# Experts: the front of a chunk runs six steps ahead instead of four

## What is computed

```python
x = x + gnn(...) + mix(...)                        # the residual x2
xf = layernorm(x)
probs = softmax(xf @ Wg + bg)                      # 8 experts
comb = probs * (probs is among the two largest)
out = 0
for e in range(8):
    h = gelu(xf @ W1[e] + b1[e])                   # 512 -> 128
    out = out + comb[:, e:e+1] * (h @ W2[e] + b2[e])   # 128 -> 512
x = x + out
```

## Time and profile before

| | |
|---|---|
| three runs | 2988.32 us median (2987.90 to 2995.39) |
| the profiled execution | 2990.87 us |
| its span in the profile | 2989.3 us |
| busy in the span | PE 2588.8, PEld 2119.4, DVE 1641.8, ACT 1326.5, POOL 1121.3 us |
| mean granted TensorE clock | 0.944 |

### The profile page before, as it was taken

How to read it: one execution, slowest core, us unless ns; L and a number is a source line. 1 busy time by engine, 2 the same in 40 slices (tenths; PEclk the granted TensorE clock), 3 DMA queues, 4 the chain that set the end, 5 groups by cost and what they waited for, 6 DMA issues and landing times.

```text
span 2989.3 us, 78905 instructions
## 1 busy us (share of the span) xinstructions
PE 2588.8 (87%) x32457; PEld 2119.4 (71%) x32457; DVE 1641.8 (55%) x3354; ACT 1326.5 (44%) x3694; POOL 1121.3 (38%) x1128
## 2 busy tenths in 40 slices
PE   5989998999999999589897788888888589589998
PEld 4867886888887888465686677777776465477776
DVE  5225777666666666647313455555555646666643
ACT  3323443656565655322331465665555322334432
POOL 0000001777776767100001477777777211122110
PEclk8999999999999999899998899999999889699998
DMA  5662013999999999540126599999999641122211
GB/s 198 229 266 101 36 54 105 354 355 356 350 358 343 357 340 346 177 129 2 71 95 233 210 345 352 349 351 356 354 345 351 208 118 52 39 96 92 71 64 57
DMA packets 233911, 647.37 MB, mean 217 GB/s; under 512 B 39072, under 2 KB 45856, under 8 KB 231491
## 3 DMA queue, kind: packets, MB, share of 16 engines
q0 software_dynamic: 137088, 466.78, 42.9%
q1 hardware_dynamic: 96451, 175.38, 17.1%
HBM read 551.60 MB, written 116.19 MB: 223 GB/s over the span
## 4 chain that ended last, share of the span: by engine, by line
PE 68%; DMA 15%; DVE 7%; issue 5%; POOL 2%; ACT 2%; SPq 1%; POOLq 0%; DVEq 0%; ACTq 0%
PE ps L1282 10%; PE ps L1312 5%; PE ps L1325 5%; DMA Y<-KVd,srcE 5%; PE ps L595 4%; PE ps L596 4%; PE ps L597 4%; DMA xT<-KVd,srcE 3%; PE ps L1289 3%; PE ps L1006 2%; PE ps L1008 2%; PE ps L1007 2%; DMA Qd<-stage 2%; PE ps L1966 2%; PE ps L1968 2%
## 5 line engine op out<-in xcount | busy, mean ns | idle before, releaser
L1189 POOL DMA_INDIRECT Y<-KVd,srcE x356 | 341.1, 958 | 132.7 <-issue 63.9
L1189 POOL DMA_INDIRECT xT<-KVd,srcE x225 | 214.6, 954 | 312.6 <-DVE xs L1053 195.4
L1482 ACT ACTIVATE stage<-ps,stage 128x128 f32<-128x128 f32 x832 | 294.9, 367 | 32.8 <-PE ps L1289 29.8
L1463 ACT ACTIVATE work<-ps 128x512 f32<-128x512 f32 x309 | 180.4, 597 | 285.6 <-PE ps L1282 285.3
L595 PE MATMUL ps<-Wh,xs 128*128 128x512 f32 x600 | 240.3, 400 | 55.4 <-DVE xs L535 55.4
L1463 ACT ACTIVATE G<-ps 128x512 f32<-128x512 f32 x315 | 183.4, 597 | 233.2 <-PE ps L1282 232.8
L1382 DVE COPY G<-ps 128x512 f32<-128x512 f32 x208 | 143.9, 692 | 259.5 <-PE ps L1289 251.0
L1282 PE MATMUL ps<-ident,Y 128*128 128x128 f32 x1424 | 201.6, 280 | 42.7 <-DMA Y<-KVd,srcE 34.3
L596 PE MATMUL ps<-Wl,xs 128*128 128x512 f32 x600 | 238.1, 397 | 0.0
L597 PE MATMUL ps<-Wh,xs 128*128 128x512 f32 x600 | 237.9, 396 | 0.0
L1189 POOL DMA_INDIRECT WA<-KVd,srcE x120 | 116.8, 974 | 318.7 <-PE ps L597 276.4
(11 more groups left out here) (403 smaller groups left out, 6884.3 us busy)
## 6 DMA issues: line engine op xcount, KB each, us to landing
KVd<-stage SPq DMA_DIRECT2D x96, 256.0 KB, 2.0
xTd<-xT SPq DMA_DIRECT2D x2, 6250.0 KB, 26.4
xT<-xTd SPq DMA_DIRECT2D x2, 6250.0 KB, 26.4
aggd<-work SPq DMA_DIRECT2D x6, 2048.0 KB, 7.4
Qd<-stage SPq DMA_DIRECT2D x48, 256.0 KB, 2.0
G<-aggd SPq DMA_DIRECT2D x48, 256.0 KB, 2.7
Y<-in_x SPq DMA_DIRECT2D x4, 1536.0 KB, 14.5
G<-mixq SPq DMA_DIRECT2D x24, 256.0 KB
```

The source lines that it names most:

```text
L1189: pool.indirect_dma_start(out=kvs[a], out_offset=None, in_=KVd[l][:, :], in_offset=bass.IndirectOffsetOnAxis(ap=srcE[:, n:n + 1], axis=0)) ...
L1463: act.activation(kT[n % len(kT)], banks(l)[place_of(l, "k", n) % len(banks(l))][:, :], ACT.Copy).then_inc(out_a, 1)
L1482: last = act.activation(pT[g % len(pT)][:, P * i:P * (i + 1)], SC[g % 2][:, P * i:P * (i + 1)], ACT.Exp, bias=smin[:, t:t + 1], scale=-1.0 ...
```

## The change

One number: `AHEAD`, the steps of chunk 1's front that every engine takes before unit 0, goes from 4 to 6.

```diff
-        UNITS, STEPS, AHEAD = 8 * NCK, 24, 4
+        UNITS, STEPS, AHEAD = 8 * NCK, 24, 6
```

## The result

| | before | with the change |
|---|---|---|
| median of 17 runs | 2988.67 us (2980.43 to 2995.39) | 2998.0 us (2991.13 to 3004.25) |
| ratio, with 95% interval | | 1.0029 (1.0020 to 1.0037) |
| profiled execution | 2990.87 us | 2991.24 us |
| its span | 2989.3 us | 2989.7 us |
| PE busy in it | 2588.8 us | 2580.5 us |

What follows compares the result with a forecast made beforehand. TensorE was taken to bound the stage, leaving only its waits to win. -8.0 + 4.7 - 1.9 - 3.1 + 3.0 = -5.3 us from the profiled 2990.9 gives 2985.6; the median lies 2.6 lower: 2983.0 us, range 2974 to 2993.

Steps and rivals of the forecast that it cites:

- The seam: Between chunks, from `up` to the first downs: L2689's 2.0 us wait goes in four chunks, -8.0 us.
- The square root: Before `hidH` of row 0: its table load fits before VectorE's sums, without drain, so `hidH` doesn't wait.
- The residuals: Before row 2's downs: the chain delays `hidL`, so TensorE waits 3.1 us instead of about 1.9; sum +4.7 us.
- the "1.5" for the fourth residual: On VectorE, between `weigh` and two statistics before `hidL` of row 2: the fourth residual takes 1.5 us.
- The clock: Downs behind the row-2 waits: two of four possible 1.5 us stretches at 1.2 GHz, +3.0 us.
- Row 3 and the gate: Waits for row 3's tiles shrink, -1.9 us, and waits in front of the gate go, -3.1 us.
- Rival 1: Row 2's wait stays near 2 us and the clock isn't lowered: 2976 us, chance 0.25.
- Rival 1's first condition: In row 2, GpSimd is less in the way at `weigh`: 0.69 us and not 1.75.
- Rival 2: Row 3's comb fetch lands late, TensorE waits 7 us there and is slow for 1.5: about 3014 us, chance 0.1.
- the sign named for it: `weigh` in row 3 waits for DMA for over 2 us in more than chunk 4.
- Rival 3: Longer waits lower the clock and slack before row 7 or the gate is missed: 2988 to 2992 us, chance 0.2.

Runs made afterwards that it cites:

- e1: The changed kernel with VectorE's low parts of the first two tiles a step earlier, in front of `weigh` of row 4; 2982.26 us, ratio 0.9981.
- e5: e1 with the fourth residual moved behind `hidL` of row 2 and the statistics after it; 2994.88 us, ratio 1.0012.
- e2: The changed kernel with SP issuing `fetch_comb(u + 2)` before its three steps; 2993.06 us, ratio 1.0008.
- e4: The changed kernel with only steps 0 to 6 six ahead, the rest two steps later, where they were before; 2981.15 us, ratio 0.9970.
- e6: e4 with the residuals at steps 9, 10, 12 and 13; 2977.51 us, ratio 0.9957.
- e7: e6 with the comb fetch issued before SP's steps; 2971.48 us, ratio 0.9948.
- e8: The kernel before with `AHEAD = 5`; 2976.64 us, ratio 0.9962.
- e11: e8 with the comb fetch before SP's steps, except that of a new chunk's first row; 2972.80 us, ratio 0.9928.
- e12: e11 with the fourth residual at step 11, behind `hidL` of row 2; 2976.92 us, ratio 0.9953.

## Why the prediction was wrong

The forecast was 2983.0 us, with 2974 to 2993 as range; 2998.0 was measured. By its own steps:

- **The seam: right.** -8.0 forecast, and -9.7 measured; of the excess 1.5 is the slow clock of chunk 3 that the prediction counted as gone elsewhere. L2689 takes 1.10 us.
- **The square root: right.** No wait for it at the seam, and no drain behind the loads: after the change `inner` starts 0.01 us behind the end of a load (2695.33 and 1.28, 2696.62).
- **The residuals: the mechanism right, the size not.** The 6.3 us of the chain came out, and so did the waits of chunk 2 (3.17) and chunk 4 (2.37). In chunk 0 the wait is 6.22 where 4.74 and 0.6 had been added up, and in chunks 1 and 3 it is 5.23 and 4.22 where 3.1 was forecast. In all 11.0 us of wait were added. The forecast has +4.7, which is 6.2 us of wait less the 1.5 of slow clock in chunk 3. The term mis-sized was the "1.5" for the fourth residual: from its first pass to its end it took 4.8 us in chunk 1 (1.8 and 1.75 beside GpSimd and 1.21 of wait between), and 4.8, 3.8, 3.7 and 2.6 in chunks 0, 2, 3 and 4. Part of it is the later landing of its tile (at most the 0.80 us that GpSimd waited in chunk 1); whether the comb fetch that the change had moved in front of it made that is argued and not shown. I followed the comb fetch of row 3 through SP's queue, and not that of row 2. In chunk 1 the first residual also waited, 1.08 us, for an output's store.
- **The clock: too low.** "I take two of the four" stretches at 1.2 GHz. All five waits of row 2 were followed by one, also the 2.37 us in chunk 4; together 8.4 us (19.4 less the 11.0 of wait), and not 3.0.
- **Row 3 and the gate: the step that failed.** Both gains are there: no wait for the gate, and the first turns wait once for 1.0 us. But the step costed only what stood in the list of waits before, and did not walk through the moved turns themselves. Step 16 moved from behind an `up` into the middle of the downs, and waited there for a PSUM bank, 2.5 to 2.8 us in five chunks, where the forecast had nothing. Rows 3 to 7 gave +3.5 us where -5.0 was forecast. With that wait removed (e1) they give -13.7, more than forecast; 6.3 of it lies in chunk 4, whose late comb fetch holds TensorE up for 1.1 us there instead of 4.0. How much of the rest is granted clock isn't taken apart.
- **The rivals.** None named this wait. Rival 1's first condition, `weigh` of row 2 at 0.69 us, was met in chunks 0 to 2, and the fourth residual was the slow pass instead. Rival 2 was the right kind of thing, a wait in row 3 that eats the seam's gain, by the wrong cause: its fetch holds `weigh` of row 3 for 1.2 to 2.3 us here and 3.96 in chunk 4, behind cover but for the 1.0 us that the first turns wait in chunk 4, and became the bound only in e5. So the sign named for it, over 2 us in more than chunk 4, was seen (2.19 and 2.26 in chunks 1 and 2) without its price. Rival 3 (2988 to 2992) had the lowered clock after every wait. 0.11 for slower was too little for a change that moves every step on every engine.

From -5.3: +11.7 in row 2, +8.5 in rows 3 to 7, and -1.7 at the seam give +13.2, which is the trace's +13.3.

## What to carry to other kernels

When a block of steps is moved, walk every moved step on every engine and ask of each what releases it at its new place, PSUM banks included; a step that waited for nothing before has no row in the list of waits, and is the one that is missed. A distance such as "two places" has different lengths in time: a place can hold an `up`, half of the downs, or a table load, so a change of one in a global number should be tried beside a change of two, and beside moving the one step that pays. A single queue needs the same walk, and the answer can be the next fetch rather than the one that was cured (e2).

## What was not expected of the hardware

- A fetch of the same bytes from the same queue lands later by what stands around it: `stage` tiles (L2339) landed 2.9 us after their issue in the median of before, and 4.3 after the change. The fourth tiles, 1.45 us behind the third's fetch with a comb fetch between, took 4.7 to 5.5. No run has the two so close without one between, so the share of each isn't shown. Where the pair is 2.0 to 2.1 us apart with no comb fetch between or in the 4 us ahead, ten of eleven (before, e4, e6, e7, e8, e11, e12) landed after 2.9 to 3.1 us, and the eight with a comb fetch 3.9 us ahead of the second (e11, e12) after 3.9 to 4.1.
- VectorE beside GpSimd took 1.79 and 1.75 us for passes that take 0.74 and 0.75 without it; that was known from the earlier trace rows, and it meets whichever pass stands there, so moving a pass moves the cost and doesn't remove it: in chunk 1 of e11 it was the fourth residual's first pass (1.75 us), in e12 `hidL` in its place (1.75 us).
- The last chunk, with no change of its instructions, took 7 us more or less with the granted clock of its stretch, 0.66 or 0.95, which is more than the 6.3 us by which the stages of the two profiled executions differ. Parts of a stage have to be compared before its sum is.
